# Starting a gated layer's first row tile inside the stage before it, and moving three of its weight loads

## What is computed

```python
x = x + _layernorm(_L0_attn_ref(_layernorm(x), ...))   # stage A
x = x + _layernorm(_L0_ffn_ref(_layernorm(x), ...))    # stage B
x = x + _layernorm(_L1_attn_ref(_layernorm(x), ...))   # stage C
x = x + _layernorm(_L1_ffn_ref(_layernorm(x), ...))    # stage D
```

```python
def _qlora_linear(x, wq, A, B):
    w = jnp.tile(wq, (1, 4))
    return x @ w.T + (x @ A.T @ B.T) * 0.5
gate = jax.nn.silu(_qlora_linear(x, w1q, a1, b1))
up = _qlora_linear(x, w3q, a3, b3)
out = _qlora_linear(gate * up, w2q, a2, b2)      # hidden width 2752
```

## Time and profile before

| what | value |
| --- | --- |
| median of 3 runs | 2486.54 us |
| the profiled execution's own time | 2484.96 us |
| span of the profiled execution | 2483.2 us |
| PE busy | 2176.5 us, 88% |
| DVE busy | 1392.5 us, 56% |
| POOL busy | 974.2 us, 39% |
| ACT busy | 919.7 us, 37% |
| DMA, share of 16 engines of the main queue | 29.3% |
| granted TensorE clock, mean | 0.932 |

### The profile page before, as it was taken

One profiled execution on the slowest core, in us unless ns is written; L12 is line 12 of the kernel. 1 busy time (PEld: TensorE's weight loads), 2 busy tenths in 40 slices (PEclk: granted clock), 3 DMA queues, 4 the chain that ended last, 5 costly groups with the idle time before them and its releaser, 6 DMA issues.

```text
span 2483.2 us, 30799 instructions
## 1 busy us (share of the span) xinstructions
PE 2176.5 (88%) x11008; PEld 1538.1 (62%) x11008; DVE 1392.5 (56%) x3136; ACT 919.7 (37%) x1623; POOL 974.2 (39%) x751
## 2 busy tenths in 40 slices
PE   4899973899999969789899889898887499999998
PEld 4655532788888858655555455555543287667676
DVE  7855764677677742375555555555563056553333
ACT  5644553333233322125454454454445122221111
POOL 1333553644444410016665556566656422110000
PEclk9999986899999979889999899999987699999999
DMA  5310256112122146422224522222222355334232
GB/s 162 101 59 1 72 176 218 62 69 76 68 82 81 60 147 239 101 49 53 57 70 113 162 57 74 73 67 61 54 64 64 125 196 170 130 119 169 110 111 94
DMA packets 139573, 249.27 MB, mean 100 GB/s; under 512 B 26890, under 2 KB 69770, under 8 KB 139196
## 3 DMA queue, kind: packets, MB, share of 16 engines
q1 hardware_dynamic: 130716, 230.51, 29.3%
q10 hardware_dynamic: 8704, 16.78, 2.1%
HBM read 139.48 MB, written 76.02 MB: 87 GB/s over the span
## 4 chain that ended last, share of the span: by engine, by line
PE 55%; POOL 16%; issue 5%; DVE 5%; DMA 3%; ACT 3%; SPq 2%; POOLq 0%; ACTq 0%; DVEq 0%
POOL c_S L2081 13%; PE PS L2264 4%; PE PS L2221 4%; PE PS L2222 4%; PE PS L2225 4%; PE PS L1024 3%; PE PS L1732 3%; PE PS L1025 3%; PE PS L1026 3%; PE PS L1716 3%; PE PS L1747 3%; PE PS L1057 2%; PE PS L1058 2%; PE PS L1059 2%; PE PS L1692 2%
## 5 line engine op out<-in xcount | busy, mean ns | idle before, releaser
L1881 ACT ACTIVATE c_P<-PS 128x512 f32<-128x512 f32 (+3 forms) x768 | 356.2, 493 | 386.6 <-PE PS L1732 341.0
L2081 POOL TENSOR_TENSOR c_S<-c_S,c_P 128x2048 f32<-128x2048 f32 (+1 forms) x96 | 337.2, 3512 | 12.9 <-ACT c_P L1881 6.7
L1716 PE MATMUL PS<-c_K,c_Q 96*128 96x512 f32 (+3 forms) x768 | 282.8, 379 | 52.5 <-DVE cst L1998 31.2
L1732 PE MATMUL PS<-c_Q,c_K 97*128 97x512 f32 (+3 forms) x768 | 295.8, 398 | 10.7 <-ACT c_P L1881 6.1
L1732 PEld LDWEIGHTS PS<-c_Q,c_K 97*128 97x128 f32 x768 | 155.3, 204 | 186.3 <-issue 83.4
L1994 DVE TENSOR_REDUCE cst<-PS 128x1 f32<-128x512 f32 x256 | 176.3, 689 | 136.5 <-PE PS L1716 136.2
L2064 POOL TENSOR_SCALAR_AFFINE_SELECT c_P<-c_P 128x512 f32<-128x512 f32 x128 | 85.3, 667 | 356.3 <-ACT c_P L1881 356.3
L1716 PEld LDWEIGHTS PS<-c_K,c_Q 96*128 96x128 f32 x768 | 157.9, 206 | 100.0 <-DVE cst L1998 49.9
L1747 PE MATMUL PS<-c_P,c_V 128*32 128x512 f32 (+3 forms) x1536 | 183.0, 551 | 38.5 <-POOL c_P L2064 26.6
L1998 DVE CUSTOM_DVE_ANT_0 PS<-PS,maskw 128x128 f32<-128x128 f32 (+3 forms) x256 | 126.9, 510 | 124.1 <-PE PS L1716 123.6
L199 POOL TENSOR_TENSOR maskw<-maskw,mhalf 128x1 f32<-128x1 f32 x64 | 36.8, 574 | 357.9 <-DVE maskw L168 357.9
(11 more groups left out here) (276 smaller groups left out, 4803.6 us busy)
## 6 DMA issues: line engine op xcount, KB each, us to landing
a_xin<-in_x SPq DMA_DIRECT2D x32, 512.0 KB, 4.3
c_Q<-c_qh SPq DMA_DIRECT2D x256, 64.0 KB, 2.0
d_x<-scr SPq DMA_DIRECT2D x32, 512.0 KB, 3.9
scr<-a_xin SPq DMA_DIRECT2D x16, 512.0 KB, 5.6
scr<-a_hid SPq DMA_DIRECT2D x16, 512.0 KB, 2.9
b_xn<-scr SPq DMA_DIRECT2D x16, 512.0 KB, 5.6
b_x<-scr SPq DMA_DIRECT2D x16, 512.0 KB, 4.8
scr<-b_x SPq DMA_DIRECT2D x16, 512.0 KB, 2.6
```

The source lines that it names most:

```text
L1716: e.matmul(bank[:, 0:hi - lo], self.Q4[0:96, 4 * (o % 3) + g, 128 * t:128 * t + 128], self.K4[0:96, HEADS[o % 8], lo:hi], start=True, stop ...
L1732: e.matmul(self.k.bank(i % 3)[:, 0:hi - lo], self.K4[0:97, HEADS[o % 8], 128 * kt:128 * kt + 128], self.Q4[0:97, 4 * (o % 3) + g, lo:hi], ...
L1881: e.activation(self.P[:, R % 3, g, 0:hi - lo], self.k.bank(i % 3)[:, 0:hi - lo], ACT.Exp, scale=SCALE).then_inc(self.exp_s.s, 1)
L2081: e.tensor_tensor(S[:, :, 512 - n:512], before[:, :, 512 - n:512], P[:, :, 0:n], ADD).then_inc(self.psum_s.s, 1)
```

## The change

Stage B's steps for its tile 0 (names beginning with b_) become steps of stage A's plan, and stage B's loops begin with tile 1. Each engine's loop in stage A gets a branch that calls first_pe, first_act, first_dve or first_pool, which call the same functions as before with t = 0. Six of the twelve low halves of w13 go to GpSimd, six stay on VectorE; the low halves of w2 are divided between VectorE and GpSimd, one of each after each of the first three chunks of tile 1. The memory layout puts a2 over the rotation tables' first three layers. The bank pairs of the last four tiles change. Transfers are issued at other places of SyncE's list.

```diff
-            self.cosT, self.sinT = sb("cosT", [128, 4, 1024]), sb("sinT", [128, 4, 1024])
+            tables = sb("tables", [128, 4, 2, 1024])
+            self.cosT, self.sinT = tables[:, :, 0, :], tables[:, :, 1, :]
...
     def out_pair(t):
-        return t % (t // 4 + 1) if t >= 8 else t % 2 if t >= 4 else 0
+        return (2, 0, 1, 3)[t - 12] if t >= 12 else t % 3 if t >= 8 else t % 2 if t >= 4 else 0
...
-        add("in", 8.0, ("nextb", 0), ("xn_", 11), ("affine", 3, 8))
+        layers = "affine", 3, 8
...
-            add("act", 2.0, ("nexth", c), ("nexth", c - 1) if c else None, *over)
+            add("act", 2.0, ("b_whi", c), ("b_whi", c - 1) if c else None, *over)
             for half in range(2):
-                add("dve", 1.15, ("nextl", 2 * c + half), ("nexth", c), ("nextl", 2 * c + half - 1) if c + half else None)
-        add("act", 3.0, ("nextbh", 0), ("nextb", 0), ("nexth", 5))
-        add("dve", 3.1, ("nextbl", 0), ("nextbh", 0), ("nextl", 11))
+                i = 2 * c + half
+                add("pool" if c < 3 else "dve", 2.35 if c < 3 else 1.15, ("b_wlo", i), ("b_whi", c),
+                    ("b_wlo", i - 1) if i not in (0, 6) else None)
+        for c in range(3):
+            add("in", 2.0, ("b_ldb", c), layers)
+            add("act", .95, ("b_bhi", c), ("b_ldb", c), ("b_bhi", c - 1) if c else None)
+            add("dve", 1.15, ("b_blo", c), ("b_bhi", c), ("b_blo", c - 1) if c else None)
+
+        for t in range(2):
+            add("in", 3.0, ("b_ldn", t), ("b_tr", 1) if t else None, layers)
+            for u in (2 * t, 2 * t + 1):
+                add("pe", .5, ("b_tr", u), ("b_ldn", t), ("b_xt", u - 1) if u % 2 else ("b_lowd", 0) if t else ("y", 12))
+                add("act", .65, ("b_xt", u), ("b_tr", u), *((("b_fold", 0), ("b_xsum", 0)) if u == 2 else ()))
...
+            add("pool", 2.1, ("b_xsum", t), ("b_xt", 2 * t + 1), ("b_xlo", 0) if t else None)
+            add("act", .45, ("b_xhi", t), ("b_xsum", t))
+            add("dve", .45, ("b_xlo", t), ("b_xhi", t))
...
+        for c in range(6):
+            add("pe", 3.0, ("b_up", c), ("b_xlo", 0), ("b_lowd", 0), ("b_blo", c // 2), ("b_wlo", 2 * c + 1), ("b_wlo", 5),
+                ("b_up", c - 1) if c else None, ("b_gate", c - 2) if c > 1 else ("y", 13 + c))
+            add("act", .6, ("b_silu", c), ("b_up", c), *((("b_acc", c - 3), ("b_gf", c - 3)) if c > 2 else ()))
+            add("dve", .7, ("b_gate", c), ("b_silu", c))
+            add("dve", 1.6, ("b_acc", c), ("b_gate", c), ("b_acc", c - 1) if c else None)
+            add("pool", 1.1, ("b_gf", c), ("b_gate", c), ("b_gf", c - 1) if c else ("b_blo", 1))
...
-            way[key] = steps[key][1] + .15 + max(map(to_end, needed[key]), default=0)
+            way[key] = steps[key][1] + .15 + max(map(to_end, needed[key]), default=0) + (12 if key == ("affine", 3, 5) else 0)
...
         self.then.sp_w13(e)
+        e.wait_ge(*self.conv(max(self.nth["conv", q, 2] for q in range(4))))
+        self.then.sp_a2(e)
         for t in range(NT):
             T.sp_store_x(e, t)
             T.sp_store_xn(e, t)
             if t + 4 < NT:
                 T.sp_load(e, t + 4)
-            if t == 11:
+            if t == 8:
                 e.wait_ge(*self.affine(self.nth["affine", 3, 8]))
                 for u in (6, 7):
                     e.wait_ge(*k.sty[u % 2](T.stores(u)))
                 self.then.sp_first(e)
-            if t == 14:
+            if t == 10:
                 self.then.sp_xn(e, 1)
+            if t == 12:
+                e.wait_ge(*self.omm(NT))
+                for u in (10, 11):
+                    e.wait_ge(*k.sty[u % 2](T.stores(u)))
+                self.then.sp_w2(e)
+            if t == 13:
+                self.then.sp_xn(e, 2)
         T.sp_end(e)
...
-        e.dma_start(self.a2[:, :], io["a2"].partition_broadcast(128)).then_inc(self.lda.s, 16)
+
+    def sp_a2(self, e):
+        e.dma_start(self.a2[:, :], self.k.io["a2"].partition_broadcast(128)).then_inc(self.lda.s, 16)
+
+    def sp_w2(self, e):
+        e.dma_start(self.w2[0:115, :, :], self.k.io["w2x"].rearrange("(c p) n -> p c n", p=115)).then_inc(self.ld2.s, 16)
...
-        for i in range(2):
-            e.dma_start(self.w2[0:115, 3 * i:3 * i + 3, :], io["w2x"].rearrange("(c p) n -> p c n", p=115)[:, 3 * i:3 * i + 3, :]
-                        ).then_inc(self.ld2[i].s, 16)
-        self.sp_xn(e, 2)
...
-                e.wait_ge(*k.y_yn(first.T + 15))
+                e.wait_ge(*k.y_yn(first.T + 13))
...
-                    for i in range(2 * c, 2 * c + 2):
-                        self.pool_wlo(e, i)
+                    self.w2lo(e, 2 * c)
```

More of the change, by code:

```diff
@@ L933, in __init__ @@
          self.low_s, self.lowc_s, self.lowd_s, self.up_s, self.silu_s, self.gate_s, self.gf_s, self.u2_s, self.u2r_s,
          self.gtr_s, self.ghi_s, self.glo_s, self.down_s) = k.sigs(
-            "b_", "whi wlo bhi blo w2hi w2lo tr xt fold usb xsum xhi xlo low lowc lowd up silu gate gf u2 u2r gtr ghi glo down")
+            "b_", "whi wlop wlod bhi blo w2hi w2lo tr xt fold usb xsum xhi xlo low lowc lowd up silu gate gf u2 u2r gtr ghi glo down")
         self.tail = Tail(k, [x[:, :] for x in self.xr], [y[:, :] for y in self.yr], x_src, x_dst, xn_dst)
@@ L1060, in pe_down, with first_pe @@
         m.then_inc(self.down_s.s, 1)
-    def pe(self, e):
[L1063 to L1067, removed]
+    def first_pe(self, e, name, i):
+        if name == "b_tr":
+            self.pe_trans(e, i // 2, i % 2)
+        elif name == "b_fold":
+            self.pe_fold(e, i)
+        elif name == "b_low":
+            self.pe_low(e, i)
+        else:
+            self.pe_up(e, 0, i)
+    def pe(self, e):
+        for t in range(1, NT):
             for c in range(6):
                 self.pe_up(e, t, c)
-                if t > 0 and c in (0, 2):
+                if c in (0, 2):
                     self.pe_gtr(e, t - 1, c // 2)
@@ L1143, in act_ghi, with first_act @@
                ).then_inc(self.ghi_s.s, 1)
+    def first_act(self, e, name, i):
+        if name == "b_whi":
+            self.act_whi(e, i)
+        elif name == "b_bhi":
+            self.act_bhi(e, i)
+        elif name == "b_xt":
+            self.act_xt(e, i // 2, i % 2)
+        elif name == "b_usb":
+            self.act_usb(e, i)
+        elif name == "b_xhi":
+            self.act_xhi(e, i)
+        elif name == "b_lowc":
+            self.act_low(e, i)
+        else:
+            self.act_silu(e, 0, i)
     def act(self, e):
         T, y = self.tail, self.k.bank(6, 2)
[L1147 to L1152 removed]
+        for t in range(1, NT):
             for c in range(6):
@@ L1169, in act @@
                     T.act_x(e, t - 2)
-                if t > 0 and c == 5:
+                if t == 1 and c == 5:
+                    first = self.first.tail
+                    for u in (14, 15):
+                        e.wait_ge(*self.k.sty[u % 2](first.stores(u)))
+                if c == 5:
                     T.act_y(e, t - 1, y)
@@ L1238, in dve @@
         own = self.k.mine["dve"].on(e)
-        self.dve_xlo(e, 0)
-        self.dve_low(e, 0)
-        for t in range(NT):
+        for t in range(1, NT):
             for c in range(6):
-                if t > 0 and c == 5:
+                if c == 5:
                     e.wait_ge(*self.down_s(2 * t))
@@ L1306, in pool_gf, with first_pool @@
         e.tensor_tensor(self.gf[:, c, 0:m], self.g2[:, 0:m], self.g2[:, m:2 * m], ADD).then_inc(self.gf_s.s, 1)
+    def first_pool(self, e, name, i):
+        if name == "b_wlo":
+            self.wlo(e, i).then_inc(self.wlop_s.s, 1)
+        elif name == "b_xsum":
+            self.pool_xsum(e, i)
+        else:
+            self.pool_gf(e, 0, i)
     def pool(self, e):
         T = self.tail
-        self.pool_xsum(e, 0)
-        for t in range(NT):
+        for t in range(1, NT):
             for c in range(6):
-                if t > 0 and c == 5:
+                if c == 5:
                     T.pool_y(e, t - 1)
```

134 lines of the change are left out of this document (85 added, 49 removed).

## The result

| | kernel before | changed kernel |
|---|---|---|
| median of 20 runs each | 2483.85 us (2476.67 to 2488.61) | 2478.76 us (2472.37 to 2483.10) |
| ratio | | 0.998, 95% interval 0.9971 to 0.9988 |
| profiled execution | 2484.96 us, span 2483.2 | 2481.49 us, span 2479.8 |

The gain is 5.1 us by the medians, 3.5 by the two profiled executions, where 16 were forecast. It is small, but the interval excludes 1.

The account below looks back on a forecast made before the run. TensorE's own work was taken to bound the kernel, with only waits at the joint of stages A and B movable. Tile 0's 5 us plus tile 1's 11 us made 16 us off: median 2470.5 us, range 2445 to 2484.

Parts of the forecast that it names:

- First loads: Stage B's first loads, moved from t = 11 to t = 8, delay y of tile 11 from 371.66 to about 377.
- Banks: Tile 12's output uses tile 11's bank pair, so waits for y of tile 11; y of tile 12 at 387.5.
- The queue at t = 10 and group 3's order: SyncE waits for tile 0's transposes, free at 391.5; group 3's order gains 3 us (bounds 0 and 8); w2 at 396.
- w2: w2, issued at t = 12 on five DMA engines, holds tile 13's stores; y of tile 15 at 426 instead of 409.05.
- Tile 0 within stage A: Tile 0's chunks around y of tile 15: last silu at 443, 5 us before 447.88.
- Tile 1: Stage B's tile 1: w2's 18.80 us wait goes, subtractions are divided; 3 of 13.94 us excess left, gain 11 us.
- a2: a2's load leaves the joint, going out before the first store; removes the 14.76 us store wait as it stands.
- The first (full gain): Nothing holds tile 0, as w2 uses all engines or silus precede y of tile 15: 41 us, 2445.5; chance 0.16.
- The second rival: Group 3's order gains 8 us or y of tile 11 is not delayed; w2 at 388, 2458 to 2462; chance 0.12.
- The third: GpSimd's new subtractions hold VectorE's scale or nm steps, 8 us on the chain: 2478.5; chance 0.09.
- w13's halves: Six subtractions move from VectorE (1.11 us each) to GpSimd (about 2.4 each); effect taken as 0.
- The fourth (slower): SyncE's waits push w2 to 412 and y of tile 15 precedes tile 0's copies: 9 us slower, 2495.5; chance 0.09.

Follow-up runs that it names:

- taking the stall away: Changed kernel with w2 loaded as two transfers, rows 0 to 111 and 112 to 114, at the same queue place: 2466.18 us, ratio 0.9932.

## Why the prediction was right or wrong

**What bounds the kernel, and the sign: right.** TensorE's work is unchanged, only the joint moved, and it moved down. The median lies inside the range of 2445 to 2484, but that is the range's width: only a third of the forecast gain came. Of the two terms of the sum, tile 0's 5 us came to 0.1 and tile 1's 11 us to 4.5.

**First loads: right.** y of tile 11 at 377 was forecast, bounds 373 and 380; it came at 379.25. **Banks: right.** y of tile 12 at 387.5; 388.61. The prediction carried this delay of 8 to 10 us on to w2, but did not ask what it costs: issuing the same loads one tile later is worth 8.9 us.

**The queue at t = 10 and group 3's order: 8 us short.** I took w2 at 396, of which 3 us was a gain in group 3. There was none: its last affine step came at 366.65 against 366.92. And SyncE was free of the transposes at 394.70 instead of 391.5. They ended at 393.4, and until 393.86 SyncE also waited for tile 10's normalised rows, which ScalarE's new order puts behind the copy of tile 0's first transpose:

```profile
392.11 0.58 ACT L1163 COPY b_xT<-PS 128x512 f32<-128x512 f32 x1 [1.45 <-PE PS L1031]
392.59 1.24 ACT L220 ACTIVATE a_hid<-a_xin,maskw 128x1024 f32<-128x1024 f32 x1
```

In the kernel before, their store had gone out at 376.63. w2 went out at 403.89.

**w2: the wait right, its price too high.** 30 us from w2's issue to y of tile 15 were forecast, 31.9 measured, and the signs named for it (a long wait on a store's landing, a DMA share of about 0.3) stand in the rows. That the number fits so well is in part luck: the sum took the store to go out right behind w2, and it went out 17.6 us later. Without any w2 in front, y of tile 15 still comes at 424.16 (w2 behind all stores), so w2's width explains 11.6 of the 26.7 us between 409.05 and 435.79. The rule of the Trainium skill, "DMA: Bandwidth & Descriptors", section "Why a DMA increments its semaphore by 16 and not by 1", gave five engines for 115 partitions in one transfer as in two; the trace agrees, with 27.9 us from issue to use where w2 stood behind all stores against up to 28.4 before, and the share of 0.89 once its rows are 112 and 3.

**"Tile 0 within stage A": the step that failed first.** It forecast tile 0's last silu at 443 and counted 5 us as gain. The silu came at 437, earlier than forecast and outside the 440 to 446 named as its sign, because the plan put four silus ahead of y of tile 15. Yet nothing was gained, because the milestone was the wrong one. While tile 0 ran alone on the engines, its end was tile 1's start; once it is woven into stage A's order, tile 1 starts when its own inputs are ready, and xlo(1) stood in VectorE's order behind tile 15's statistics and the late products. Moving that one item forward gave 5.1 us, taking the stall away gave 12.6.

**"Tile 1": the larger error, 11 us forecast, 4.5 measured.** The step read "w2 is there in time, so the wait of 18.80 goes". It did go, and was worth nothing: the kernel before without it ran at a ratio of 1.0002. Under it lay the second path, six low halves one after another on GpSimd, and the "issue" of 6.75 us before the first down was the wait for the last of them; after the change it is 6.49. Dividing them is worth the 4.5 us and, when undone, takes back the whole change. The low clock, which I had counted as shrinking, was only moved: it now follows the 16.27 us before tile 1. By the prediction's own mark, tile 1 counted from tile 0's last silu (436.89) took 48.8 us (42.44 before), over the 37 that it had named as a sign of being wrong.

**a2: counted as gone, was shadowed.** The 14.76 us were worth 2.9 us in the kernel before, hardly more than nothing by the interval, and 7.3 with w2 out of the way.

**The rivals.** The first (full gain) needed w2 on all engines or y of tile 15 behind the silus. The second condition came true for four of six silus, and did not help, for the reason above; the first, made by hand, gave 12.6. The second rival needed w2 at 388. The later first loads take the delay from y of tile 11 and bring w2 to 393.62 and the time to 2469.88, where it had said 2458 to 2462. The third said that GpSimd's new subtractions hold VectorE. Steps side by side do lengthen each other where it could be seen: 0.63 becomes 2.12 for a product and 2.40 becomes 3.34 for a subtraction in tile 1, in line with the exclusion that the Trainium skill's "SBUF — State Buffer", section "Who interferes with whom", states; but there the change took such work away from GpSimd. The move of w13's halves was not tried alone. Its six subtractions on GpSimd ran from 298.48 to 330.24, though, and the last affine step behind them came no later than before (366.65 against 366.92), so the trace shows no cost of it in the joint. The fourth (slower) set its point at w2 at 404, and w2 went out at 403.89. Its time did not come: w2 was 8 us short of the 412 it reckoned with, and y of tile 15 was not ahead of tile 0's copies, the second condition that it named.

## What to carry to other kernels

A wait in the chain shows where time passed, not what its removal gives: ask what ends next, and remove two suspected parallel waits together before judging either. When a step is woven into an earlier stage, recompute whose readiness starts the step after it; its inputs may now stand behind unrelated late work in an in-order engine. And for a transfer in front of others in one queue, look at how many DMA engines it uses: w2 in 115 rows cost 12.6 us in front of the stores and 17 us more behind them, and in 112 and 3 rows it could stay where it was. A wait that the profile calls "issue" may be one for another engine: compare its end with what ends just before it.

## What the runs showed of the hardware

A transfer of 115 partitions held up what stood behind it in its queue: the 512 KB store that y of tile 15 waits for landed 31.9 us after w2's issue and 14.3 after its own, the last part of it at a DMA share of 0.25, where with w2 behind it or in 112 and 3 rows it took about 3. SyncE itself was held 11.75 us in the issue right behind w2 (405.23), against 0.45 with w2 in 112 and 3 rows. And slowing has two sides: the GpSimd subtraction and the VectorE product lengthen each other, by up to 0.94 and 1.5 us; six on VectorE alone did no better than three and three.
